# Two softplus additions of a selective-scan kernel moved from GpSimd to accumulating DMA transfers

## What is computed

```python
dt = softplus(einsum('blr,er->ble', dt, dt_proj_w) + dt_proj_b)
A = -exp(A_log)
def step(h, inp):
    dt_t, B_t, C_t, x_t = inp
    dA = exp(dt_t[:, :, None] * A)
    h = dA * h + (dt_t * x_t)[:, :, None] * B_t[:, None, :]
    y = einsum('bds,bs->bd', h, C_t)
```

## Time and profile before

| | us |
|---|---|
| median of 3 runs (17285.9 to 17292.63) | 17287.28 |
| the profiled execution's own time | 17281.15 |
| its span | 17279.2 |
| PE busy | 14535.6 (84%) |
| DVE busy | 14988.9 (87%) |
| ACT busy | 11261.9 (65%) |
| POOL busy | 14970.7 (87%) |
| DMA packets of SP's queue | 42.8% of 16 engines' span |

### The profile page before, as it was taken

The page is one execution under the profiler, slowest core; times in us unless marked ns, Lnnn a source line. Parts: engine busy times, 40 slices in busy tenths (PEclk is TensorE's granted clock), DMA queues, the critical chain, the costliest instruction groups (busy, mean ns, idle before and its releaser), DMA issues. The chain is left out here.

```text
span 17279.2 us, 159098 instructions
## 1 busy us (share of the span) xinstructions
PE 14535.6 (84%) x30720; PEld 5796.6 (34%) x30720; DVE 14988.9 (87%) x13132; ACT 11261.9 (65%) x18548; POOL 14970.7 (87%) x6268
## 2 busy tenths in 40 slices
PE   6888878888788887888878888788887888878888
PEld 2333333333333333333333333333333333333333
DVE  7999969999699996999969999699996999869998
ACT  4667657676566765667656666566665666656675
POOL 5999969999699996999969999699986999869998
PEclk8999989999899998999989999899998999989999
DMA  3444434444344443444434444344443444434443
GB/s 130 155 156 160 156 108 156 154 159 157 111 154 156 158 154 115 155 154 158 152 116 157 152 157 156 114 154 156 156 154 118 157 153 154 151 118 152 152 152 135
DMA packets 739059, 2535.91 MB, mean 147 GB/s; under 512 B 77240, under 2 KB 78016, under 8 KB 721728
## 3 DMA queue, kind: packets, MB, share of 16 engines
q1 hardware_dynamic: 738112, 2527.45, 42.8%
HBM read 2376.15 MB, written 150.99 MB: 146 GB/s over the span
## 5 line engine op out<-in xcount | busy, mean ns | idle before, releaser
L1200 POOL TENSOR_TENSOR RING<-RING,CS 128x1024 f32<-128x1024 f32 x4096 | 9832.9, 2419 | 1054.6 <-DVE RING L921 1037.3
L921 DVE TENSOR_TENSOR_SCAN RING<-DA,HS,RING 128x512 f32<-128x512 f32 x8192 | 9948.9, 1264 | 785.1 <-ACT DA L649 528.7
L369 PE MATMUL YP<-RING,EYE 128*128 128x512 f32 x16384 | 8378.6, 643 | 1931.3 <-POOL RING L1200 1899.3
L649 ACT ACTIVATE DA<-ITEM,AN 128x512 f32<-128x512 f32 x8192 | 5526.7, 685 | 3369.3 <-DVE RING L921 3359.7
L369 PEld LDWEIGHTS YP<-RING,EYE 128*128 128x128 f32 x16384 | 3122.7, 199 | 6731.5 <-issue 3495.4
L901 DVE TENSOR_TENSOR RING<-DTP,BS 128x1024 f32<-128x1024 f32 x2816 | 3374.9, 1206 | 0.2 <-DMA BS<-bc_rows 0.2
L1187 POOL TENSOR_TENSOR RING<-ITEM,BS 128x1024 f32<-128x1024 f32 x1280 | 3019.4, 2360 | 8.6
L369 PE MATMUL FL<-XN,WC 128*128 128x512 f32 x4096 | 1954.3, 622 | 48.1 <-ACT XN L734 36.6
L1205 POOL TENSOR_TENSOR ITEM<-ITEM,EX 128x1024 f32<-128x1024 f32 x256 | 602.6, 2354 | 1048.7 <-ACT EX L703 1048.7
L369 PEld LDWEIGHTS FL<-XN,WC 128*128 128x128 f32 x4096 | 847.4, 207 | 1194.5 <-issue 1151.3
L662 ACT ACTIVATE ITEM<-FL,COL 128x512 f32<-128x512 f32 x512 | 347.9, 680 | 1202.1 <-PE FL L369 1202.1
(11 more groups left out here) (122 smaller groups left out, 10420.8 us busy)
## 6 DMA issues: line engine op xcount, KB each, us to landing
BS<-bc_rows SPq DMA_DIRECT2D x2048, 512.0 KB, 4.9
CS<-bc_rows SPq DMA_DIRECT2D x2048, 512.0 KB, 3.6
XR<-in_x SPq DMA_DIRECT2D x128, 1024.0 KB, 7.4
x_slices<-XR SPq DMA_DIRECT2D x64, 1024.0 KB, 8.0
XR<-x_slices SPq DMA_DIRECT2D x64, 1024.0 KB, 7.4
out<-XR SPq DMA_DIRECT2D x64, 1024.0 KB, 7.9
ITEM<-in_wqkv SPq DMA_DIRECT2D x24, 1024.0 KB, 5.5
bc_rows<-ROWS SPq DMA_DIRECT2D x256, 64.0 KB, 4.5
```

The lines of the kernel that those rows point to most:

```text
L369: return pe.matmul(*a, **k)
L649: act.activation(DA[:, h, :], DT[:, i % 2, h, :], ACT.Exp, scale=AN[:, h, s:s + 1]).then_inc(dA_ready, 1)
L921: dve.tensor_tensor_scan(H[:, slot(n), h, :], DA[:, h, :], U[:, slot(n), h, :], HS[:, i % ITEMS, h, s:s + 1], ALU.mult, ALU.add).then_inc( ...
L1200: pool.tensor_tensor(G[:, slot(n)], H[:, slot(n)], CS[:, s % C_ROWS, :].unsqueeze(1).broadcast_to([P, NH, T]), ALU.mult).then_inc(g_ready, 1)
```

## The change

`dt_first` and `dt_sum` become DMA transfers, SBUF to SBUF, that add their source to the destination. POOL issues them; each adds 16 to its semaphore when it has landed. `dt_sum` moves from behind the product of step 10 (+ d) to behind that of step 11 (+ d), `dt_x` from 11 to 12, ACT's `dtx_copy` from 13 to 14. The waits for `large_ready`, `dt_begun` and `poly_ready` stand ahead of the product G of the step, not at the transfer. In windows of kind 3 the U of state 0 moves behind `dt_x`. At an image's start two small products (128 x 2 elements) carry the waits.

```diff
@@ scalar
-                    act.wait_ge(dt_ready, tile * ITEMS + i + 1)
+                    act.wait_ge(dt_ready, tile * (16 * ITEMS) + 16 * (i + 1))
...
-                        if s == 13 + d:
+                        if s == 14 + d:
                             dtx_copy(tile, w + 1)
@@ gpsimd
+            def dt_first(i):
+                pool.dma_start(DT[:, i % 2], EX[:, :, :], accum_op=ALU.add).then_inc(dt_begun, 16)
+
+            def dt_sum(i):
+                pool.dma_start(DT[:, i % 2], YZ[:, :, :], accum_op=ALU.add).then_inc(dt_ready, 16)
 
             def dt_x(tile, i):
-                pool.wait_ge(dt_ready, tile * ITEMS + i + 1)
+                pool.wait_ge(dt_ready, tile * (16 * ITEMS) + 16 * (i + 1))
...
+                    u_ahead = (n + U_LEAD) % NS in POOL_U and (front or s < NS - U_LEAD)
+                    if u_ahead and not (d and s == 13):
                         make_u(tile, n + U_LEAD, first=first)
+                    if front and s == 9 + d:
+                        pool.wait_ge(large_ready, tile * ITEMS + w + 2)
+                    if front and s == 11 + d:
+                        pool.wait_ge(dt_begun, tile * (16 * ITEMS) + 16 * (w + 2))
+                        pool.wait_ge(poly_ready, tile * ITEMS + w + 2)
                     out_state(tile, n, first=first)
...
-                        if s == 9 + late(j):
-                            dt_first(tile, w + 1)
-                        if s == 10 + late(j):
-                            dt_sum(tile, w + 1)
-                        if s == 11 + late(j):
+                        if s == 9 + d:
+                            dt_first(w + 1)
+                        if s == 11 + d:
+                            dt_sum(w + 1)
+                        if s == 12 + d:
                             dt_x(tile, w + 1)
+                    if u_ahead and d and s == 13:
+                        make_u(tile, n + U_LEAD, first=first)
 
             with pool.Fori(0, BATCH) as b:
-                dt_first(b * NT, 0)
-                dt_sum(b * NT, 0)
+                pool.wait_ge(large_ready, b * (NT * ITEMS) + 1)
+                pool.tensor_tensor(DTX[:, :, 0:1], AN[:, :, 0:1], AN[:, :, 0:1], ALU.mult).then_inc(sums_open, 1)
+                dt_first(0)
+                pool.wait_ge(dt_begun, b * (16 * NT * ITEMS) + 16)
+                pool.wait_ge(poly_ready, b * (NT * ITEMS) + 1)
+                pool.tensor_tensor(DTX[:, :, 1:2], AN[:, :, 0:1], AN[:, :, 0:1], ALU.mult).then_inc(sums_open, 1)
+                dt_sum(0)
+                pool.wait_ge(sums_open, b * 2 + 2)
                 dt_x(b * NT, 0)
```

More of the change, by code:

```diff
@@ L155, in block_ssm_kernel @@
             sem(n) for n in ("u_dve", "u_pool", "dA_ready", "scanned", "g_ready", "state_kept", "g_summed"))
-        rows_ready, rows_stored, capped = (sem(n) for n in ("rows_ready", "rows_stored", "capped"))
+        rows_ready, rows_stored, capped, sums_open = (sem(n) for n in ("rows_ready", "rows_stored", "capped", "sums_open"))
         b_landed = tuple(sem(f"b_landed_{n}") for n in range(B_ROWS // 2))
@@ L1227, in window @@
                 j = w % ITEMS
+                d = late(j)
                 ahead = tile + w // ITEMS
@@ L1230, in window @@
                     n = w * NS + s
-                    if (n + U_LEAD) % NS in POOL_U and (front or s < NS - U_LEAD):
+                    u_ahead = (n + U_LEAD) % NS in POOL_U and (front or s < NS - U_LEAD)
+                    if u_ahead and not (d and s == 13):
                         make_u(tile, n + U_LEAD, first=first)
+                    if front and s == 9 + d:
[3 more added lines that the diff above has]
+                        pool.wait_ge(poly_ready, tile * ITEMS + w + 2)
                     out_state(tile, n, first=first)
```

## The result

| | before | after |
|---|---|---|
| median | 17286.89 us | 18893.42 us |
| runs | 17285.9 to 17292.63 | 18873.57 to 18900.5 |
| ratio | | 1.0927 [1.0908, 1.0946] |

Slower by 9.3%, 1607 us, where 739 were forecast. The direction held and the time lies in the range, in the case called the long landing; the forecast itself missed by 873 us.

What follows compares the result with a forecast made beforehand. DVE and POOL were taken to bound the kernel by turns; later windows (672 us) plus image starts (67 us) made 739 us on 17281.15, so 18020 us, 4.3% slower. The range was 17230 to 19000 us.

Steps and rivals of the forecast that it cites:

- the long landing: Rival, chance 0.20: adding or POOL's descriptors are slow; a transfer taking 8.6 us gives 19009 us, 10 us gives 19728.
- What bounds the kernel: Steady tiles: DVE and POOL hand the pace to each other once per window; POOL is behind until the gate.
- POOL's saved time is worth nothing in the changed order: Steps 11 to 15: the saved 4.7 us per window becomes waiting ahead of dt_x; step 15's product ends 0.8 us later.
- I assume that kinds 0 and 3 behave as kind 1: Price per window: 3.2 us later in each of the 23 windows of kinds 0, 1 and 3 per image.
- nothing in the change makes DVE earlier there: Scans of steps 11 and 12: they still end at 7750.62 and 7754.76, so POOL must wait for them.
- L = 6.5: Time in us from POOL reaching a transfer to its landing: 6.15, the middle of 4.9 and 7.4, plus 0.35 for issue.
- free times of 6.8 and 4.1 us: First transfer costs nothing up to 6.8 us, second up to 4.1; beyond 6.8 each further us counts twice per window.
- Kind 2's absorbed 1.9 us: Eight windows per image: third U ends 1.9 us ahead of its scan, so only 1.3 us is paid.
- The image's start: Before DVE's first scan: 15.7 us instead of 7.3, so 8.4 later, 67 us for 8 images.
- beside and not on top: ACT's copy: dt_x 5.5 us later, copy 3.9 later, leaving 1.6 us that doesn't add to the window's 3.2.
- the short landing: Rival, chance 0.14: transfers take at most 4.1 us, giving 17448 us, or 17224 if ACT's copy stops waiting.
- The relief rival: Chance 0.09: gate and scans stop waiting for POOL, 16702 us; needs transfers under 3.4 us and step 12's scan by 7754.0.

Runs made afterwards that it cites:

- both transfers short: Changed kernel, SP issuing its C and B loads of steps 12 to 15 only after each transfer has landed, in kinds 0 to 2: 17662.41 us.
- the run of the moves: Changed kernel's order with both sums made by POOL additions instead of transfers: 17780.42 us.
- The plain ones: Changed kernel with both transfers lacking accum_op, so they overwrite dt instead of adding: 17835.81 us.

## Why the prediction was right or wrong

**What bounds the kernel: right.** DVE and POOL hand the pace to each other once per window, so a delay of POOL behind step 11 reaches the gate. `dt_x` waited for the landing, the gate and ACT's copy waited longer, as listed.

**POOL's saved time is worth nothing in the changed order: held up.** With both transfers short, the kernel is still 2.2% slower. But the reason given covers only part. The moves were priced at 0.8 us later, in kinds 0, 1 and 3 alike. With POOL's additions the run of the moves shows 0.5 in kind 0, 3.7 in kind 1, where the polynomial is shut out longer, and 3.1 in kind 3, where DVE waits for `HS`; "I assume that kinds 0 and 3 behave as kind 1" failed. The moves with no landing at all cost 493 us, where 0.8 a window made 147. The polynomial was in no step of the working, though it stood in the trace with durations from 1.2 to 6.3 us. In the changed kernel its whole-run median is 1.2 us instead of 2.2, since no `dt_first` runs beside it. So "nothing in the change makes DVE earlier there" was wrong: in the earlier trace rows's window the polynomial, 2.44 us long, stands right ahead of the scan of step 11. With that wait gone, kind 1 still pays 2.1 where the pair is held, and no run shows why. The two scan ends in the working (7750.62, 7754.76) stand 0.08 ahead of those that the earlier trace rows give; nothing hangs on it.

**L = 6.5: the step that failed.** Its upper end, 7.4, came from a plain 1 MB load. The transfer lands after 8.3 to 8.5 us (medians) in kinds 0 to 2, and L is some 0.25 more: 8.6 instead of 6.5, outside the interval from 4.9 to 7.4 at its top. In kind 3 and at the starts it lands after 4.6, L = 4.8, just under the interval: one L for all places was wrong too. POOL's part in L, bounded by nothing and 3.5, is 0.87. Two factors were seen one at a time, and their product was not: "the second sum meets exactly that pair" stands in the working, the adding stands in the rival, and the runs show that each is dearer with the other. The place where the pair meets the *first* sum too was used only for the rival, though SP's timeline before showed it as plainly.

**What was built on L: right in form for kinds 0 and 1, and near in the sum in part by luck.** In the earlier trace rows's kind of window the first transfer is reached at 7639.7 and released the product at 7648.25, L = 8.55; the second from 7650.6 to 7659.5, L = 8.95. By the formula that is 3.2 + (8.95 - 6.5) + (8.55 - 6.8) = 7.4 us, against 7.9 measured for kind 1. With the medians of the landings, L = 8.7, kind 0 comes to 7.3 against 7.0. So the free times of 6.8 and 4.1 us, and the double count beyond 6.8 for the first sum, are borne out there. With the landings as measured the same arithmetic gives 7.3, 7.2, 5.3 and 1.5 us for kinds 0 to 3 and 4.9 for a start, by estimate 1390 us in all and not 1607. That 19009, the sum at L = 8.6, lies near 18893 is luck: it charges kind 3 with 7.05 where 2.2 was paid, and kind 2 with 5.15 where 8.0 was. The kernel with both transfers short measured 17662 where the arithmetic at L = 4.9 has 17616, but with 0.8, 2.1, 0.6 and 2.4 us in kinds 0 to 3 where it has 1.6, 1.6, 0 and 1.6.

**Kind 2's absorbed 1.9 us: wrong.** With its landings kind 2 would have paid 5.3 by the formula; it paid 8.0, as much as kind 1. DVE waits there 11.3 us a window for `DA` (4.0 before) and 1.3 for POOL's U (none before), so the delay did not come through U and the gate alone, where the slack was read. With the copy moved out of the way these waits only change places and the interval stays. The cause is open; where the landing is short kind 2 pays 0.6.

**Kind 3: overpriced by its L, underpriced by the rest.** 3.2 was charged for L = 6.5, 2.2 paid. For the landing of 4.6 the formula gives 1.5; the 0.7 above it are not separated from the moves, which cost 3.1 in this kind with POOL's additions.

**The image's start: overpriced.** 8.4 us each was forecast. DVE's first scan of an image starts 4.7 us later than before, and at the next polynomial 3.1 of that are left. The start of the first image shows both transfers landing alone:
```profile
174.05 1.03 POOL L1204 DMA_DIRECT2D ITEM<-EX  x1
178.85 0.19 POOL L1258 TENSOR_TENSOR ITEM<-AN 128x2 f32<-128x2 f32 x1 [3.77 <-DMA ITEM<-EX]
178.99 0.86 POOL L1207 DMA_DIRECT2D ITEM<-YZ  x1
183.62 2.33 POOL L1211 TENSOR_TENSOR ITEM<-ITEM 128x1024 f32<-128x1024 f32 x1 [3.77 <-DMA ITEM<-YZ]
```
From the first small product at 173.91 to the first U at 186.03 it is 12.1 us, not 15.7: the two 6.5 were 4.7. The earlier trace rows had 7.3.

**ACT's copy, "beside and not on top": right**, though its wait grew by 5.3 us per item (1665 us in all against 299) and not by 1.6: with the copy later still, the time stays within 0.1%. The 224 us that the short landing added for a copy that no longer waits, on which the lower end of the range rests, are worth nothing: with that wait down to 53 us the kernel before is no faster.

**The relief rival: its condition was not enough.** The accumulating transfers never landed under 4.4 us, so for them it could not happen. The plain ones of kind 3 landed after 3.0, L = 3.2 and under the 3.4 that was asked, and their interval was still 2.1 us longer than before; whether the scan of step 12 was in time there was not read. In the old order, where only one sum leaves POOL and nothing waits for it before a product of 3.2 us has passed, there is a gain of 203 us; whether it is POOL's relief or the polynomial's is open.

## What to carry to other kernels

A transfer that replaces an instruction must be priced where it starts: look which loads wait for the same event, since they will start with it and share its engines. Price an accumulating transfer beside other loads from neither a plain one nor one alone. And before giving the idea up, move the loads, not the transfer: here the ones that collided had 5 us of room, and using it turned a loss of 2.6% into a gain of 1.1% with one sum as a transfer, and a loss of 9.3% into one of 2.2% with both. Look also at what else the replaced instruction held off: here the polynomial on DVE.

## What was not expected of the hardware

- An accumulating transfer of 512 KB from SBUF to SBUF takes 4.5 to 4.7 us alone and 8.3 to 8.5 beside two loads of 512 KB; a plain one 3.0 and 5.7. The fit of the Trainium skill (DMA: Bandwidth & Descriptors, section Anatomy of one DMA) gives 3.2 for this size: it agrees with the plain transfer alone and with no other cell.
- The sharing works both ways: B's loads beside a transfer landed after 8.1 us (median), the others after 4.9.
- POOL is held 0.87 us (median) by an issue, 0.70 to 1.03, with landings from 4.5 to 9.3.
- DVE's polynomial with both inputs in SBUF takes 1.2 us, 2.4 when it starts beside `dt_first`, and up to 6.3 beside POOL instructions without a gap; where it is held off, it ends some 1.1 us after a POOL instruction does. What that costs or gives back in the time was not measured by itself.
